# VectorE's order in the late cross and feed-forward slots

## The reference

```python
h = layernorm(x + multihead(x, x, x, causal=True), ln1_g, ln1_b)
h = layernorm(h + multihead(h, ctx, ctx, causal=False), ln2_g, ln2_b)
ff = relu(h @ ff_w1.T + ff_b1) @ ff_w2.T + ff_b2        # hidden width 1024
x = layernorm(h + ff, ln3_g, ln3_b)
# layernorm: gamma * (x - mean) / (std + 1e-6) + beta, std over d - 1
q, k, v = x @ Wq + bq, ctx @ Wk + bk, ctx @ Wv + bv
w = softmax(q @ k.T / 16)
g = concat(q, w @ v) @ Wg + bg
out = (w @ v) * mask * sigmoid(g) + x
```

## Time and profile before

| | |
|---|---|
| median of 3 runs | 870.49 us (865.95 to 873.68) |
| the profiled execution, its own time | 876.23 us |
| its span in the profile | 874.4 us |
| TensorE products busy | 787.5 us, 90% |
| VectorE busy | 663.4 us, 76%, 1503 instructions |
| GpSimd busy | 485.7 us, 56% |
| ScalarE busy | 438.1 us, 50% |
| mean granted TensorE clock | 0.952 |
| L1649, VectorE's tile | 128 of 0.48 us; idle before them 27.5 us |

### The profile page before, as it was taken

How to read it: one execution, slowest core, us unless ns; L and a number is a source line. 1 busy time by engine, 2 the same in 40 slices (tenths; PEclk the granted TensorE clock), 3 DMA queues, 4 the chain that set the end, 5 groups by cost and what they waited for, 6 DMA issues and landing times.

```text
span 874.4 us, 19926 instructions
## 1 busy us (share of the span) xinstructions
PE 787.5 (90%) x7232; PEld 652.9 (75%) x7232; DVE 663.4 (76%) x1503; ACT 438.1 (50%) x907; POOL 485.7 (56%) x598
## 2 busy tenths in 40 slices
PE   5897899999999998788889999999999889999885
PEld 4676777777777775555558888888877779889874
DVE  3535767767776988667889989998888775977774
ACT  4431255555565555555555555555544543545442
POOL 2401366677667675563446666566545665667542
PEclk9997999999999999889789999999999997999978
DMA  8397588867775766336342222222200020011222
GB/s 269 60 358 170 101 144 141 146 103 130 136 125 98 116 98 120 77 84 121 63 92 47 59 53 53 52 53 54 53 2 10 1 70 8 28 54 58 77 81 76
DMA packets 105296, 79.58 MB, mean 91 GB/s; under 512 B 43255, under 2 KB 101961, under 8 KB 104941
## 3 DMA queue, kind: packets, MB, share of 16 engines
q1 hardware_dynamic: 101434, 72.02, 40.1%
q10 hardware_dynamic: 3764, 6.29, 2.0%
HBM read 27.03 MB, written 12.97 MB: 46 GB/s over the span
## 4 chain that ended last, share of the span: by engine, by line
PE 59%; DVE 18%; issue 6%; ACT 3%; SPq 2%; DMA 2%; POOL 1%; POOLq 0%; DVEq 0%; ACTq 0%
PE a_misc L87 13%; PE a_pair L87 11%; PE a_s L1004 7%; PE a_pair L793 3%; PE a_pair L965 3%; PE a_s L769 3%; PE a_pair L950 3%; PE a_pair L811 3%; PE a_s L767 3%; PE a_s L927 2%; PE a_pair L1103 2%; PE a_s L87 2%; DVE a_rest L1422 2%; ACT a_parts L1141 1%; DVE c_z L1511 1%
## 5 line engine op out<-in xcount | busy, mean ns | idle before, releaser
L1407 DVE TENSOR_REDUCE a_nm<-a_s 128x2 f32<-128x512 f32 (+1 forms) x192 | 127.4, 679 | 57.3 <-PE a_s L769 55.6
L1920 POOL TENSOR_TENSOR c_hidden<-c_hid,c_hidden 128x256 fp32r<-128x256 f32 x128 | 95.9, 749 | 119.8 <-DVE c_hid L1649 119.4
L1170 ACT ACTIVATE a_pT<-a_pair 128x512 f32<-128x512 f32 x192 | 113.8, 597 | 94.3 <-PE a_pair L793 88.0
L1265 ACT ACTIVATE a_pT<-a_pair 77x512 f32<-77x512 f32 x128 | 76.0, 594 | 142.5 <-PE a_pair L950 138.1
L1004 PE MATMUL a_s<-c_w,c_hidden 128*128 128x256 f32 x768 | 119.2, 295 | 0.0
L87 PE MATMUL a_pair<-c_fxh,c_w 128*128 128x256 f32 x512 | 101.7, 291 | 13.8 <-DVE c_hid L1649 13.8
L1827 POOL TENSOR_SCALAR_AFFINE_SELECT a_pT<-a_pT 128x256 f32<-128x256 f32 (+1 forms) x192 | 91.8, 496 | 30.2 <-ACT a_pT L1170 29.7
L1004 PEld LDWEIGHTS a_s<-c_w,c_hidden 128*128 128x128 f32 x768 | 100.7, 193 | 0.4 <-issue 0.4
L87 PEld LDWEIGHTS a_pair<-c_fxh,c_w 128*128 128x128 f32 x512 | 80.0, 193 | 16.8 <-DVE c_hid L1649 16.7
L1649 DVE TENSOR_SCALAR c_hid<-a_pair,ff_b_col 128x256 f32<-128x256 f32 x128 | 61.3, 479 | 27.5 <-ACT c_hidden L1291 27.2
L793 PE MATMUL a_pair<-a_sq,a_sk 98*128 98x256 bf16 (+1 forms) x512 | 75.9, 252 | 6.6 <-ACT a_pT L1170 6.5
(11 more groups left out here) (258 smaller groups left out, 2157.3 us busy)
## 6 DMA issues: line engine op xcount, KB each, us to landing
a_sq<-a_parts SPq DMA_DIRECT2D x96, 128.0 KB, 4.3
a_sk<-a_parts SPq DMA_DIRECT2D x96, 128.0 KB, 4.6
a_sq<-c_parts SPq DMA_DIRECT2D x96, 128.0 KB
x<-in_xT SPq DMA_DIRECT2D x16, 256.0 KB, 5.9
res<-in_x SPq DMA_DIRECT2D x16, 256.0 KB, 5.6
out<-g_fin SPq DMA_DIRECT2D x16, 256.0 KB, 2.1
a_sk<-kc_parts SPq DMA_DIRECT2D x96, 38.5 KB
fold_rows<-x_fold ACTq DMA_DIRECT2D x1, 2496.0 KB, 11.3
```

The lines of the kernel that those rows point to most:

```text
L1170: nc.scalar.activation(pT[g % NPT][:], stps[g % 2][:], ACT.Exp).then_inc(s_exp, 1)
L1265: nc.scalar.activation(pT[g % NPX][0:SC], st_ps[0:SC, :], ACT.Exp).then_inc(c_exp, 1)
L1407: nc.vector.tensor_reduce(nm[c % 2][:, QT * heads[0] + qt:QT * heads[-1] + qt + 1:QT], sps[g % 2][:].rearrange("p (h k) -> p h k", h=len(h ...
L1920: nc.gpsimd.tensor_tensor(hl(m), hid[n % NHID][:], f32(hh(m)), ALU.subtract).then_inc(c_hl, 1)
```

## The change

In some slots VectorE issues its feed-forward tile `hidden` right behind `cross_maxes` (and, in slot 7, `feed_residual`), ahead of whatever else stood between: the residual, the two norms' deviation steps and the centring. These slots are all those of rounds 15 and later, and slots 3, 4 and 6 of rounds 10 and 14. `feed_deviation` asks the same question as before through a new helper; what it does stays.

```diff
+    ends_group = lambda c: any(c == r[-1] for r in feed_groups)
...
             def feed_deviation(c, step):
-                if not real(c) or c != feed_groups[group_of(c)][-1]:
+                if not ends_group(c):
                     return
...
             def cross_slot(n, s):
                 g = V * n + s
+                tile_first = n >= B - 1 or s in (3, 4, 6) and ends_group(n - 7)
                 if s == 7:
                     feed_residual(n - 6)
                 cross_maxes(n, s)
+                if tile_first:
+                    hidden(g - UP_LAG - 1)
                 if s == 3:
                     cross_residual(n - 3)
...
                 if s in (6, 7):
                     deviation(n - 3, s - 6)
-                hidden(g - UP_LAG - 1)
+                if not tile_first:
+                    hidden(g - UP_LAG - 1)
                 if s == 0:
                     cross_turn_av(n - 2, 0)
```

## The result

The changed kernel took **886.5 us** (median of 4 runs, 884.38 to 887.26), the kernel before 868.65 us in the same comparison (4 runs, 865.95 to 873.68). The ratio is 1.0159, 95% interval 1.0114 to 1.0205: slower, where 867.0 was forecast, and outside the range of 860 to 876. A second comparison gave 884.58 against 869.05 us, 1.0186 (1.0137 to 1.0234).

A forecast was written before the change was run, and what follows sets the result against it. TensorE was taken as the bound nearly everywhere, with VectorE mattering only where TensorE waits for it or such a stop lowers the clock. -3.0 - 1.7 + 5.0 + 3.2 = 3.5 us gained: 870.5 - 3.5 = 867.0 us, range 860 to 876.

The forecast's parts named there:

- the other four waits: TensorE's tile waits at 566.42, 745.49, 768.75 and 789.74 us: 3.2 us gained (0.2, 1.0, and 2.0 for the last two).
- slot 0 of rounds 15 to 17: Tile waits of 1.05, 0.92 and 1.96 us bring no gain; 3.0 us lost, plus 1.7 us by low clock.
- the string: VectorE's work up to L1587 in slot 0, rounds 15 to 17: ends 0.8 us later in round 15, 3.0 lost in all.
- L1602 behind four refining steps and the stop, together an estimated 1.0 us: Round 16: L1602, last of slot 7, is 1.0 us later, and so is ScalarE's half, beside 0.8 carried.
- one stop of 0.6 us a slot: Each slot with small steps: the first slips through, the second stands behind GpSimd's subtraction; 0.6 us charged.
- Slots 3, 4, 6 and 7 without a wait cost nothing.: Reordered slots without a tile wait cost 0, as the moved steps' results are read a slot or a round later.
- One more short stretch: After rounds 15 to 17's waits, one more 3.3 us low-clock stretch at half speed: 1.7 us lost, bounds 0 and 4.9.
- a stop of 1 us: Round 18, slot 0: with a 1 us stop in place of 2.82, the low clock should not come.
- Slot 0 of round 18: Tile first gains 2.8 us up to the projection and 2.2 behind it by clock: 5.0, bounds 2.8 and 7.7.
- The full clock from 721.3 to 731.6: Sign of being right: clock full from 721 to 731, where the kernel before had 0.50 after a 2.82 us wait.
- The slower one: Rival, chance 0.20: hole in VectorE's string, slot 0 of rounds 15 to 17; 7.9 us slower, 878.4, up to 883.3.
- The prediction's 1 us for that: If a slipped-in small step holds up GpSimd's subtraction, by at most 0.15 us, the sum is 1 us or so worse.

The follow-up runs named there:

- Experiment 6: Late deviations' eleven small steps replaced by one reciprocal, against the kernel before (872.78 us): new order 864.95 us (0.9911), old order 858.71 us (0.9855).
- experiment 1: Tile first in one group of rounds alone, against the kernel before: rounds 10 and 14 0.9991, rounds 15 to 17 1.01, rounds 18 on 1.0024.
- experiment 5: Tile first in rounds 15 to 17 only, against the kernel before: slots 3, 6 and 7 alone 872.28 us (1.0015), slot 0 alone 875.82 us (1.0031).
- 7: Tile first only in slots 0 and 6 of round 18 and slot 4 of round 20, against the kernel before: 868.69 against 869.05 us, 0.9991.
- 3: Changed kernel with small steps and centring issued a slot later from round 15 on, at the next slot's end: 880.71 us, 1.0138 of the kernel before.
- 8 (c): Changed kernel with small steps and centring delayed from round 15 on to the next slot's head, behind gated work: 881.9 us, 1.0113 of the kernel before.

## Why the prediction was wrong

**What bounds the kernel.** Right in kind: TensorE's work did not change (787.6 us), and all of the loss is waits and clock. But the sum treated VectorE as the bound only where TensorE waited for it. Experiment 6, 14 us faster without the late small steps where those waits are 12.8 us in all and 5.4 of them stay, shows that it limits the late rounds elsewhere too. One reading was off: in the earlier trace rows slice 21 of the clock row has an 8, so the later half is not at 9 throughout up to the 34th. Nothing in the sum used it.

**Where the 11.7 us went.** The forecast was 3.5 us gained, the profiles are 8.2 us apart the other way. By the ledger: rounds 15 to 17 lost 8.1 us, where 4.7 was set; round 18 up to slots 3 to 5 gained 2.3, where 5.0 was set; and the other four waits, set at 3.2 gained, lost 4.9 with the slots around them (2.5 in rounds 10 and 14, 2.4 from slot 6 of round 18 to round 21). The other four are the largest miss, 8.1 us. The rest is 1.9 us by which the two executions differ by themselves, less 0.7 behind round 21.

**Waits change their name in slot 0 of rounds 15 to 17.** Right mechanism, wrong size. Predicted: 3.0 us lost and 1.7 by clock, 4.7. Measured: +1.8, +4.9 and +1.4 in the ledger, 8.1. Split at the start of each projection, 4.4 us are the string and 3.7 us come behind it, where the low clock is. In round 15 the string's 0.8 held: it measured 0.6. The term of the string that failed is **"L1602 behind four refining steps and the stop, together an estimated 1.0 us"** in round 16, with what was carried into it. L1603 was to end at 675.2 and ended at 677.83, 2.6 later. Of these, 1.0 is the steps: 2.0 us later where 1.0 was set, since the charge was one stop of 0.6 us a slot, and there were two in a row (0.72 and 1.22 us) as GpSimd went from its subtraction to `a_ol`.

The other 1.6 is what came in from before, +2.4 in place of +0.8. Of that +2.4 the string of round 15 is 0.6, the stretch with the low clock at 659.2, which the forecast set a round later, 1.1, and what rounds 10 and 14 had left 0.6 (2.5 lost, 1.9 hidden by the difference of the two executions). From there on the estimate held: L1613 ended 2.5 later than set (682.64 against 680.1), and the projection started 2.5 later (685.25 against 682.7).

**"Slots 3, 4, 6 and 7 without a wait cost nothing."** This step failed in the traces. Rounds 10 and 14, counted as 0.2 us gained, lost 1.1 and 1.4 in the changed kernel and 2.5 by themselves in experiment 1, though its timed runs show no loss (0.9991). `feed_residual` was held up in the string and TensorE's down product waited 2.2 us for it (in five pieces, where the kernel before has no such wait). In rounds 15 to 17 slots 3, 6 and 7 cost next to nothing alone (1.0015, 1.1 us in the trace), but the traces of experiment 5 show that they and slot 0 are not additive. I had looked only at who reads the moved steps' result, not at what stands behind them on the queue.

**The clock.** One more short stretch was forecast; there were 23.9 us of low clock in place of 13.6 by 805 us, and 27.3 by 820. I also wrote that a stop of 1 us should bring none; 3.4 us came at 734.2, behind stops of 2.38 us (at 729.02) and 1.14 us (at 733.49). Beyond the profiles, about half of the timed loss goes with a mean clock of 0.946 to 0.955 in all runs of the changed kernel, where the kernel before had up to 0.971. The sum was made against one execution at 0.952 and had no term for it. The long stretch at 721 was itself a thing of that execution: the profile of rounds 10 and 14 alone, with the old order there, has 3.4 us in its place.

**Slot 0 of round 18.** Predicted 5.0 us: 2.8 up to the projection and 2.2 behind it by the clock. Experiments 1 and 7 gain 3.0 at the up product, but only 2.2 is left at the projection, which stood still 2.67 us in both; the changed kernel has 1.4 left there. Behind the projection 0.9 to 1.1 us were gained in all three, where 2.2 was set: the low clock did not go, it got shorter (3.4 us in each). The full clock from 721.3 to 731.6, set down as a sign of being right, holds for the changed kernel but lies over earlier work. The ledger has 2.3. So the wait changed its name here too, from the tile to the projection: L1588, which it needs, is behind the small steps, the centring and the tile. Just before, in slot 7 of round 17, VectorE of the changed kernel:

```profile
725.62 0.74 DVE L1992 SCALAR_TENSOR_TENSOR a_root<-a_prod,a_root 128x2 f32<-128x2 f32 x1
726.39 1.19 DVE L1994 SCALAR_TENSOR_TENSOR a_prod<-a_root 128x2 f32<-128x2 f32 x1
...
727.58 0.68 DVE L1736 TENSOR_TENSOR g_xl<-a_misc,g_xh 128x512 fp32r<-128x512 f32 x1
...
728.36 0.61 DVE L1729 TENSOR_TENSOR g_p<-g_p,g_rec 128x154 f32<-128x154 f32 x1
```

The same pair of stops as in round 15, and now `g_p` of a gated slot behind it; TensorE waited 2.38 us for it at 729.02.

**The other four waits.** 3.2 us were forecast. The tile's waits went (12.8 to 1.2), but from round 18 to 21 the ledger goes +6.5, +7.5, +5.4, +8.9. I wrote that only the third norm's steps move there and that nothing like the string hangs on them. The gated work does. VectorE in round 20, and TensorE's product that follows:

```profile
800.23 0.48 DVE L1650 TENSOR_SCALAR c_hid<-a_pair,ff_b_col 128x256 f32<-128x256 f32 x1 [1.00 <-ACT c_hidden L1292]
...
800.81 2.03 DVE L2002 SCALAR_TENSOR_TENSOR dev<-prod,dev 128x2 f32<-128x2 f32 x1
802.88 1.14 DVE L2004 TENSOR_SCALAR dev<-dev 128x2 f32<-128x2 f32 x1
...
804.94 0.41 DVE L1742 TENSOR_TENSOR g_ptl<-a_misc,g_pth 78x256 fp32r<-78x256 f32 x1
```

```profile
805.45 0.65 PE L1047 MATMUL a_misc<-ident,res 128*128 128x128 f32 x4 [1.86 <-issue]
```

Two steps on two columns took 3.2 us, and the low part of the gated slot's turned shares (L1742) stood behind them. It reads the bank that L1047 writes, and L1047 starts 0.10 us after its end; TensorE stood still 1.86 us.

**The rivals.** The slower one had the right place and mechanism, and its condition was met: the late rounds gained less than 4.7 us. Its price of 7.9 us is close to the 8.2 us between the two profiles and the 8.1 of rounds 15 to 17, but that is in part luck: 4.9 us of it were one long low-clock stretch, where at most 3.7 us came by several, and rounds 10, 14 and 19 to 21, which it had at nothing, lost 4.9. The timed difference is twice as large. It had 0.20 and stopped at 883.3. I set it behind the forecast because the late rounds have no `cross_turn_av`; the gated stage has the same kind of consumer.

**Does a small step hold up GpSimd?** The prediction's 1 us for that didn't come. In the changed kernel GpSimd stood idle before its subtraction and a small step followed the tile at once in 12 places. The subtraction starts 0.08 us after the tile's end in all of them, as in 84 places where something else follows. The small step ends 0.07 us after the tile, before GpSimd begins. Whether one that is still running would hold it up, no run shows.

**What stays open.** Why the chip grants the same kernel 0.956 in one run and 0.971 in the next, and which share of the changed kernel's lower clock is its order. Why the last part, behind the final tile, has more low clock in experiments 3, 7 and 8 (c) (24.3 to 26.2 us in place of 19.9).

## What to carry to other kernels

When a step is moved ahead of others on an in-order queue, price every step that is now behind it, up to the next one that somebody awaits within its cover, and not only the readers of what moved. If the moved step itself waits for another engine, its wait is inserted into that string. Undoing the change slot group by slot group is worth more than summing local gains: parts of 1.0015 and 1.0031 (1.1 and 3.7 us in the traces) made 1.01 (9.3 us) together, and delaying the small steps by one slot took the 1.01 away. And a comparison product by product should rest on more than one profile of the kernel before: the one used here took 7 us more than the median run.

## What the runs showed of the hardware

A VectorE step on 128x2 takes 0.15 to 0.17 us alone and, in the lines shown, 0.72 to 2.03 us beside GpSimd, ending when an operation of GpSimd does; where GpSimd has operations back to back, successive small steps are held (0.72 then 1.22, 0.74 then 1.19, 2.03 then 1.14 us). In the first two pairs each step ends with one GpSimd operation. The 2.03 us step began with a GpSimd operation of 1.28 us (from 800.79) and ended only with the next, of 0.72 us (from 802.03). So in these places the charge was the length of GpSimd's run of work, not of one operation of it. And the mean clock granted to one unchanged kernel varied from 0.952 to 0.971 between its runs in the four comparisons, and its time with it from 877.3 to 865.5 us: 5 to 7 us for 0.01 by a line through the runs of each comparison, more than most of the effects studied here.
